# A graph, attention and expert block on one core: the SP queue's small loads go between the stores of the edge MLP's rows, and a GpSimd multiply goes ahead of the edge loop

## The reference

```
h = edge_attr_8                                   # 41250 x 8
for W in (W_mlp1, W_mlp2, W_mlp3):                # 8->64, 64->64, 64->64
    h = 1.679177 * silu(h @ W / sqrt(W.shape[0]))
w1, w2, w3, w4 = split(h @ W_mlp4 / 8, 4)         # 64 -> 512
s0, s1 = x0[src], x1[src]                         # rows of the nodes behind W_up
m0, m1 = products of w1..w4, s0, s1 and edge_attr_4
msg = segment_sum(m, dst)                         # to the nodes, then W_out
```

## Time and profile before

| | |
|---|---|
| median of 3 runs | 2283.49 us (2279.82, 2283.49, 2283.97) |
| profiled execution, its own time | 2280.27 us |
| its span in the profile | 2278.4 us |
| TensorE clock granted, mean of the span | 0.968 |
| PE busy | 2060.4 us (90%) |
| DVE, ACT, POOL busy | 1333.2, 1040.0, 617.9 us |

### The profile page before, as it was taken

One profiled execution on the slowest core, in us unless ns is written; L12 is line 12 of the kernel. 1 busy time (PEld: TensorE's weight loads), 2 busy tenths in 40 slices (PEclk: granted clock), 3 DMA queues, 4 the chain that ended last, 5 costly groups with the idle time before them and its releaser, 6 DMA issues.

```text
span 2278.4 us, 45195 instructions
## 1 busy us (share of the span) xinstructions
PE 2060.4 (90%) x13564; PEld 1487.5 (65%) x13565; DVE 1333.2 (59%) x2849; ACT 1040.0 (46%) x2316; POOL 617.9 (27%) x739
## 2 busy tenths in 40 slices
PE   5999798888888887899999999999599999879998
PEld 2544344344344346588888888888388888768886
DVE  1311588888888886655555555555612346664444
ACT  3731233333333332176777777767243223354443
POOL 2102478778777785300000000002200000000000
PEclk8999999999999999699999999999899999989999
DMA  6642367666666678444802430042700200310000
GB/s 211 222 161 89 97 189 194 187 186 188 187 192 188 180 193 323 159 179 178 306 22 78 157 115 18 18 166 63 275 15 10 84 19 19 106 42 10 10 10 18
DMA packets 157291, 288.52 MB, mean 127 GB/s; under 512 B 43533, under 2 KB 85270, under 8 KB 152615
## 3 DMA queue, kind: packets, MB, share of 16 engines
q1 hardware_dynamic: 111349, 158.80, 20.4%
q0 software_dynamic: 37552, 121.91, 18.2%
q10 hardware_dynamic: 8322, 6.89, 0.9%
HBM read 233.69 MB, written 53.85 MB: 126 GB/s over the span
## 4 chain that ended last, share of the span: by engine, by line
PE 59%; DVE 15%; DMA 9%; issue 8%; ACT 3%; DVEq 2%; POOL 2%; SPq 1%; POOLq 0%; ACTq 0%
PE psum L2540 14%; DMA big_b<-sender_table,wide 8%; PE psum L2678 6%; PE psum L2711 4%; PE psum L2530 4%; PE psum L2531 3%; PE psum L2532 3%; DVE big_b L1713 3%; PE psum L2576 3%; DVE big_b L1714 3%; PE psum L2585 3%; PE psum L2616 3%; PE psum L2606 2%; PE psum L2258 2%; POOL big_b L1034 1%
## 5 line engine op out<-in xcount | busy, mean ns | idle before, releaser
L1034 POOL DMA_INDIRECT big_b<-sender_table,wide x360 | 368.6, 1024 | 107.7 <-issue 85.0
L2389 PEld LDWEIGHTS psum<-big_b,wide 128*32 128x32 f32 x3600 | 166.4, 109 | 199.9 <-issue 136.7
L2359 PE MATMUL psum<-w_mlp,wide 64*128 64x512 f32 x728 | 207.9, 648 | 79.1 <-DVE big_b L1714 75.7
L2389 PE MATMUL psum<-big_b,wide 128*32 128x256 f32 (+2 forms) x3600 | 272.2, 390 | 4.1 <-POOL wide L1063 4.0
L2540 PEld LDWEIGHTS psum<-xn_T,big_b 128*128 128x128 f32 x2048 | 262.0, 191 | 21.2 <-issue 3.2
L2540 PE MATMUL psum<-xn_T,big_b 128*128 128x128 f32 x2048 | 265.0, 275 | 0.0
L1242 ACT ACTIVATE wide<-psum 128x384 f32<-128x384 f32 x45 | 22.1, 490 | 396.3 <-PE psum L2400 396.3
L1888 DVE TENSOR_TENSOR w_lo<-wide,w_hi 128x512 fp32r<-128x512 f32 x184 | 127.3, 692 | 118.0 <-ACT w_hi L1334 118.0
L2530 PE MATMUL psum<-w_hi,hid_hi 128*128 128x512 f32 x368 | 176.0, 478 | 10.1 <-DVE w_lo L1888 7.2
L1235 ACT ACTIVATE wide<-wide 128x290 bf16<-128x290 f32 x360 | 158.6, 527 | 42.4 <-PEq L2362 37.2
L1712 DVE TENSOR_TENSOR big_b<-psum,big_b 128x512 f32<-128x512 f32 x180 | 123.8, 688 | 90.5 <-DMA big_b<-sender_table,wide 73.8
(11 more groups left out here) (453 smaller groups left out, 3947.5 us busy)
## 6 DMA issues: line engine op xcount, KB each, us to landing
big_a<-in_L_ffn_W SPq DMA_DIRECT2D x12, 2048.0 KB, 13.7
big_b<-in_L_ffn_W SPq DMA_DIRECT2D x12, 2048.0 KB, 13.6
wide<-in_L_ffn_W SPq DMA_DIRECT2D x8, 2048.0 KB, 23.5
wide<-edge_hidden SPq DMA_DIRECT2D x182, 64.0 KB
edge_hidden<-wide SPq DMA_DIRECT2D x21, 512.0 KB, 2.8
tokens_sorted<-zeros SPq DMA_DIRECT2D x29, 256.0 KB, 3.7
adj_dram<-big_a SPq DMA_DIRECT2D x1, 6400.0 KB, 22.3
xn_T<-tokens_sorted POOLq DMA_DIRECT2D x25, 256.0 KB, 2.9
```

Source lines behind the costliest of these rows:

```text
L1034: nc.gpsimd.indirect_dma_start(out=sent[q][:, j, :], out_offset=None, in_=sender_table, in_offset=bass.IndirectOffsetOnAxis(ap=indices[j], ...
L2359: last = nc.tensor.matmul(tile_w[q % 2][:, j, :], h3_slot[q][halves[j], :], w_mlp4[halves[j], :], start=True, stop=True)
L2389: nc.tensor.matmul(msg_psum[k].rearrange("p (c u) -> p c u", u=MUL)[bands[g], cols, :], hot_y[q][:, j, y, :], p[:, of, :], start=False, st ...
```

## The change

Two things change.

1. On SP the loads behind Wl leave their place ahead of the turns and go between the stores of the rows: behind the store of turn 0 `w_up`, of turn 1 the mix biases, of turn 2 the last edge inputs and their padding, of turn 3 `w_mlp4` and `w_out`, of turn 4 the two tables. The tiles of zeros start in turn 5 instead of turn 0: 36 tiles over 16 turns, three in each of turns 5 to 8 and two in the others.
2. On GpSimd the cast to `ident16` in the set-up goes. In its place, in turn 10 behind the reduction, stands a multiply of the identity with itself (the same values), which fills `ident16`. Ahead of the edge loop GpSimd waits until it is done.

The diff, with the moved loads shown once, in their new place:

```diff
+        LATE = 5
...
             for w in ("Wk", "Wv", "Wl"):
                 sp.dma_start(w_rows[w], ...)
-            sp.dma_start(w_up[:, 0, :], A["L0_gnn_W_up0"]).then_inc(loads["w_up"], 16)
...
+            def late_loads(n):
+                if n == 0:
+                    for k in range(2):
+                        sp.dma_start(w_up[:, k, :], ...)
+                if n == 1:
+                    for b in ("bk", "bv", "bl"):
+                        sp.dma_start(b_row[b][:, :], ...)
+                    sp.dma_start(bq_col[:, :], ...)
+                if n == 2:
+                    sp.dma_start(edge_in[last_turn:E, :] ...)
+                    sp.wait_ge(padding_ready, 3)
+                    for e0, n, row in PADS:
+                        sp.dma_start(edge_in[e0:e0 + n * row, :] ...)
+                if n == 3:
+                    for j in range(2):
+                        sp.dma_start(w_mlp4[HID * j:HID * j + HID, :], ...)
+                    for k in range(2):
+                        sp.dma_start(w_out[:, k, :, :], ...)
+                if n == 4:
+                    sp.wait_ge(consts_ready, 2)
+                    for tab, a, w in ((src_ids, A["src"], 1), (edge_y, ..., Y)):
+                        sp.dma_start(tab[0:FULL_ROWS, :], ...)
+                        sp.dma_start(tab[FULL_ROWS:FULL_ROWS + 1, 0:REST * w], ...)
...
                 sp.dma_start(hidden_cols[...], h3_out[a]).then_inc(h3_stored[a], 16)
+                late_loads(n)
...
-                for tile in zero_tiles[n::TURNS]:
+                for tile in zero_tiles[n - LATE::TURNS - LATE] if n >= LATE else []:
...
-            nc.gpsimd.tensor_copy(ident16[:, :], ident[:, :]).then_inc(consts_ready, 1)
             for n in range(RING, TURNS):
                 edge_inputs(n)
                 if n == 10:
                     pool.wait_ge(reach_ready, 1)
                     nc.gpsimd.partition_all_reduce(reach_all, reach, P, RMAX)...
+                    nc.gpsimd.tensor_tensor(ident16[:, :], ident[:, :], ident[:, :], ALU.mult).then_inc(consts_ready, 1)
...
             pool.wait_ge(layer_done[0], TURNS)
+            pool.wait_ge(consts_ready, 3)
```

More of the change, by code:

```diff
@@ L759, in _ @@
                 sp.dma_start(w_rows[w], A[f"L0_mix_{w}"].rearrange("(c p) d -> p c d", p=P)).then_inc(loads[w], 16)
-            sp.dma_start(w_up[:, 0, :], A["L0_gnn_W_up0"]).then_inc(loads["w_up"], 16)
[L761 to L788, removed]
+            def late_loads(n):
+                if n == 0:
+                    for k in range(2):
+                        sp.dma_start(w_up[:, k, :], A[f"L0_gnn_W_up{k}"]).then_inc(loads["w_up"], 16)
+                if n == 1:
+                    for b in ("bk", "bv", "bl"):
+                        sp.dma_start(b_row[b][:, :], A[f"L0_mix_{b}"].rearrange("(a d) -> a d", a=1).to_broadcast([P, D]))\
+                            .then_inc(loads["mix_b"], 16)
+                    sp.dma_start(bq_col[:, :], A["L0_mix_bq"].rearrange("(c p) -> p c", p=P), allow_slow_non_contiguous=True)\
+                        .then_inc(loads["mix_b"], 16)
+                if n == 2:
+                    last_turn = (TURNS - 1) * TURN_UNITS * U
+                    sp.dma_start(edge_in[last_turn:E, :].rearrange("(a b) r -> a (b r)", a=2),
+                                 A["edge_attr_8"][last_turn:E, :].rearrange("(a b) r -> a (b r)", a=2)).then_inc(loads["edge_in"], 16)
+                    sp.wait_ge(padding_ready, 3)
+                    zero_rows = zeros16[:, :].bitcast(F32)
+                    for e0, n, row in PADS:
+                        sp.dma_start(edge_in[e0:e0 + n * row, :].rearrange("(a b) r -> a (b r)", b=row), zero_rows[0:n, 0:row * R])\
+                            .then_inc(loads["edge_in"], 16)
+                if n == 3:
+                    for j in range(2):
+                        sp.dma_start(w_mlp4[HID * j:HID * j + HID, :], A["L0_gnn_W_mlp4"]).then_inc(loads["w_out"], 16)
+                    for k in range(2):
+                        sp.dma_start(w_out[:, k, :, :], A[f"L0_gnn_W_out{k}"].rearrange("(c p) v -> p c v", p=P))\
+                            .then_inc(loads["w_out"], 16)
+                if n == 4:
+                    sp.wait_ge(consts_ready, 2)
+                    for tab, a, w in ((src_ids, A["src"], 1), (edge_y, A["edge_attr_4"].rearrange("e y -> (e y)"), Y)):
+                        k = PER_ROW * w
+                        sp.dma_start(tab[0:FULL_ROWS, :], a[0:FULL_ROWS * k].rearrange("(p k) -> p k", k=k))\
+                            .then_inc(loads["edge_tables"], 16)
+                        sp.dma_start(tab[FULL_ROWS:FULL_ROWS + 1, 0:REST * w], a[FULL_ROWS * k:E * w].rearrange("(p k) -> p k", p=1))\
+                            .then_inc(loads["edge_tables"], 16)
```

## The result

The changed kernel runs in 2267.26 us, the median of 4 runs (2263.42 to 2268.74). The kernel before, measured beside it, is at 2281.98 us, the median of 4 runs (2279.82 to 2283.97). The ratio is 0.9933 with a 95% interval of 0.9922 to 0.9945. The gain is 14.7 us; forecast were 2264.0 us, in a range of 2255 to 2273, and a gain of 19.2 (a ratio of 0.9916, just outside this interval). The profiled execution shown here took 2266.87 us, 13.4 less than the 2280.27 of before.

What follows compares the result with a forecast made beforehand. PE, busy 90% of the span, was taken as the bound, with only its waits and half clock removable. -18.3 + 7.1 - 7.0 - 1.0 = -19.2 us from 2283.5 gave 2264, range 2255 to 2273.

Steps and rivals of the forecast that it cites:

- Stores right behind Wl: Turn 2: ACT's wait for the first store goes and PE regains time and clock; -18.3 us.
- Loads of turns 0 to 3: Small loads moved between SP's stores, none needed before turn 6; cost nothing.
- The tables in turn 4: Turn 7: PE stalls 4.5 us for turn 5's store behind the tables, plus 2.6 of low clock; +7.1 us.
- Tiles of zeros: Turns 5 to 8: three instead of two, 1.3 us more per turn on a queue with slack; cost nothing.
- The multiply in turn 10: GpSimd's configuration change delays turn 11's load; 4.8 us plus 2.6 of clock uncovered, nothing behind turn 7's stall.
- The head of the loop: Edge loop's start: the first hot_y and the gathers behind it come 7.1 us earlier; -7.0 us, ends -4 and -8.
- Inside the loop: Edge loop: the pair of configuration changes in each of 45 units goes; -1.0 us, ends 0 and -4.
- Rival A: Tables not the slow transfer, or done in time: no turn 7 stall, turn 10's code load uncovered; 2264.6 us, chance 0.12.
- B: The clock doesn't fall after the short stall of turn 7; -21.8 us, so 2261.7; chance 0.14.
- C: Turn 7's stall is larger, about 12 instead of 4.5 us, with SP's issuing blocked behind the tables; 2271.8, chance 0.10.
- D: Code is loaded again at the edge loop's first hot_y, so the -7.0 us falls away; 2271.3, chance 0.08.
- E: Edge loop's rhythm gets worse; at 0.7 us per unit +12.3 us, so 2295.8; chance 0.03.

Runs made afterwards that it cites:

- the kernel with 112 + 10 rows: The changed kernel with each table's load of 122 partitions cut into one of 112 and one of 10; 2264.50 us, ratio 0.9924.

## Why the prediction was right, point by point

The time of 2264.0 was near (2267.3, and 2264.7 when measured again), and each stall came in the turn where it was put. By the steps, each with what the two profiles show:

- **Stores right behind Wl**, -18.3: layer 1 of turn 5 starts 18.4 us earlier. The 1.2 us for ACT's table loads was a choice between 0 and 2.6; that it came out at 1.26 is partly luck.
- **Loads of turns 0 to 3**, nothing: no wait names them in the turns behind, right.
- **The tables in turn 4**, +7.1: from turn 5 to turn 11 the lead shrinks from 18.4 to 9.7 us (76.28 against 85.99 in the earlier trace rows), so 8.7. The wait was 5.95 instead of 4.5, the size that was off, because the store landed 2.2 us later behind the tables than 15.2 to 16.1 us and its share allow. The rest, 8.7 - 5.95 = 2.7, goes with the low clock behind it (2.6 said). Why the landing was late stays open beyond the fall of the rate to 44 to 49 GB/s. That the tables are the cause, a guess then, is shown by the kernel with 112 + 10 rows. The share of 0.13 with 122 rows, and its end with 112 + 10, is also where the trace agrees with the rule of the Trainium skill, "DMA: Bandwidth & Descriptors", section "Why a DMA increments its semaphore by 16 and not by 1".
- **Tiles of zeros**, nothing: right in cost, wrong in what they show. They fill the DMA share to 0.54 to 0.66, so the mark of 0.13 was not to be seen until they were moved away.
- **The multiply in turn 10**, nothing under the cover of turn 7: right. Without the cover it is 4.57 to 4.58 us of wait (4.8 said), in the two kernels that lack it (the multiply alone, the tables on sixteen engines).
- **The head of the loop**, -7.0: the lead grows from 9.7 to 251.26 - 234.32 = 16.9, by 7.2. The gap that moved is 7.3 us in turn 10, against the about 6 us of the Trainium skill, "GPSIMD Engine Reference", section "2.1 Instruction dispatch"; the traces stay at 6.9 to 7.6 in every kernel here, so the measured number holds.
- **Inside the loop**, -1.0: this step failed. In these two profiles it is +2.6, over all kernels nothing that can be told from the scatter of about 5 us. A pair of 11 ns rows was no ground for a gain.

The sum of the profiles is -18.4 + 8.7 - 7.2 + 2.6 = -14.3, and 0.8 more comes in behind the loop, which gives the -13.5 between the spans. Against -19.2 that is 5.7 short: 1.6 of the stall, 3.6 of the loop and 0.8 behind it, less 0.3 by which the first step and the head gave more than said. Of these the 1.6 of the stall and the 1.0 promised for the pairs are the forecast's own errors; the other 3.4, less the 0.3, are no larger than the scatter. In the second profile of the changed kernel the loop starts 17.7 us sooner than before and takes 0.4 less, and 2.2 come in behind it, 15.9 in all by its own time of 2264.38. What lies behind the start of the loop's last multiply came out between 3.3 us less and 4.9 more than in the profile of before in the kernels of this study, which do nothing different there: it is scatter too. The medians' difference of 3.3 us to the forecast can't be divided between these errors and the scatter. In part the nearness is luck: the base had come down by 1.5 us when it was measured again, from 2283.49 to 2281.98, and without that the 4.5 us by which the gain fell short would stand in the time.

Rival A was argued as an equal sum in another place. It did not happen, but the kernel with tables on sixteen engines made it happen: 2264.50, where 2264.6 was worked out. B fell, the clock does drop behind the stall; C fell, though the SP hold-up that it named was there; D fell, for the multiply starts when DVE releases it; E fell, with 606.8 us for the loop against 606.4.

## What to carry to other kernels

Where PE feeds a ring of buffers that are freed by stores, issue the first store ahead of every load that is not needed yet, and look at the number of rows of each load: behind 122 rows a store took 16 us to land, behind 112 + 10 rows 6.8 at most. When a stall is removed and the time does not move, look for one further on that it covered; here two measures were worth 0.2 and 1.7 us alone, which the intervals don't tell from nothing, and 6.3 us together. And a wait can have two causes, a late issue and a slow landing: the cure of one leaves the rest.

## What was not expected

- **The clock falls in the midst of so short a stall.** PE stopped at 60.3 and the clock went down at about 65.4 in the changed kernel, at about 66.1 after a stop at 62.3 with the zeros moved, and at about 69.8 after a stop at 67.7 in the kernel with tables on sixteen engines, whose window shows it at the lower level and the DMA engines nearly idle:

```profile
70.00:76.80 6.80, 4.50 (x25) 2.35 (x25) 2.97 (x5) 0.60 (x1) 2.22 (x3) 0.51 0.12 29
```

  In each of the three the low level lasted some 6.8 us; behind the wait of turn 11 in the kernel with the multiply alone it was 3.4 us.
- **SP's issuing is held up when more is queued while two engines are behind.** With the tiles of zeros behind the tables, a store that takes 0.4 us to issue took 3.00 (at 57.05) and two tiles of zeros 4.65; without the zeros, or with the tables at 112 + 10 rows (two tiles of zeros 2.71), the store of turn 6 was issued in 0.4. It cost nothing here, since no one waited for what stood behind.
- **The gap belongs to the first multiply behind the reduction, wherever it stands.** It was 6.9 to 7.6 us in turn 10, behind turn 20 and at the head of the loop, later multiplies had none, and the loads behind the reduction were issued without it. That it is the loading of code is the reading that fits; no row names it.
